# Reading a transposed activation tile from its SBUF copy instead of from PSUM, in an 8-core attention and FFN kernel

## The reference

```python
xn = _layernorm(x, axis=-1)                  # x: (2, 8192, 1024) f32
latent = xn @ Wc_down                        # 1024 -> 512
q  = latent @ Wq_up                          # 16 heads of 64
kv = latent @ Wkv_up                         # one shared k and v head of 64
att = softmax(causal(q k^T / 8))
s = (att v) @ Wc_proj
h = silu(xn @ wg^T) * (xn @ wu^T)            # weights int32, times 1/127; hidden 3072
g = _silu(h @ wd^T)
out = x + s * g
```

## Time and profile before

| | us |
|---|---|
| time before, median of 2 runs | 3452.53 (3451.27 to 3453.78) |
| the profiled execution's own time | 3440.83 |
| its span, slowest core (core 5) | 3439.2 |
| spans of the 8 cores | 3406.5 to 3439.2 |
| mean granted TensorE clock of the cores | 0.790 to 0.808 |

### The profile page before, as it was taken

How to read it: one execution, slowest core, us unless ns; L and a number is a source line. 1 busy time by engine, 2 the same in 40 slices (tenths; PEclk the granted TensorE clock), 3 DMA queues, 4 the chain that set the end, 5 groups by cost and what they waited for, 6 DMA issues and landing times.

```text
span 3439.2 us, 33260 instructions; the slowest of 8 cores (3406.5 to 3439.2 us)
## 1 busy us (share of the span) xinstructions
PE 2153.8 (63%) x10464; PEld 1011.4 (29%) x10464; DVE 1186.9 (35%) x1978; ACT 1307.1 (38%) x1457; POOL 414.6 (12%) x329
## 2 busy tenths in 40 slices
PE   1334645466565574775748747587575787577876
PEld 1112323222231341442225222252221442223521
DVE  3635443342433435324243242432322322421221
ACT  0111222212331332433534436444455336366455
POOL 0111212222233001000000000000000001000000
PEclk9556767776887797997879978799787799689998
DMA  5032254839576143351015300153001251011510
GB/s 89 27 54 49 37 88 60 128 71 148 60 86 113 43 119 112 69 133 42 28 39 123 100 14 26 37 130 94 13 17 42 46 148 38 14 33 33 140 44 13
DMA packets 547288, 232.14 MB, mean 67 GB/s; under 512 B 476464, under 2 KB 532784, under 8 KB 547120
## 3 DMA queue, kind: packets, MB, share of 16 engines
q1 hardware_dynamic: 429792, 186.88, 21.0%
q0 software_dynamic: 117328, 43.14, 11.8%
HBM read 241.62 MB, written 27.26 MB: 78 GB/s over the span
## 4 chain that ended last, share of the span: by engine, by line
PE 39%; DVE 20%; DMA 15%; issue 11%; ACT 10%; POOL 4%; DVEq 1%; SPq 0%; ACTq 0%; POOLq 0%
PE ps_y L553 9%; PE ps_sc L566 9%; ACT p_sb L577 8%; PE ps_u L724 5%; PE ps_u L731 4%; POOL p_sb L585 4%; PE ps_u L795 3%; DMA wu_t<-wu 3%; DMA wd_t<-wdbf 3%; DVE recbf L605 3%; DMA xt<-xb 3%; DMA wd_t<-wd 2%; PE ps_u L643 2%; DVE xnT_own L390 2%; DVE stat L302 2%
## 5 line engine op out<-in xcount | busy, mean ns | idle before, releaser
L577 ACT ACTIVATE p_sb<-ps_sc 128x1024 bf16<-128x1024 f32 x1088 | 1088.9, 1022 | 1556.4 <-PE ps_sc L566 1549.8
L553 PE MATMUL ps_y<-p_sb,vaug_sb 128*65 128x512 bf16 x2176 | 758.5, 434 | 244.7 <-POOL p_sb L585 143.4
L566 PE MATMUL ps_sc<-qs,kT_sb 65*128 65x512 bf16 x2176 | 755.3, 433 | 26.9 <-DVE qs L534 26.9
L585 POOL TENSOR_TENSOR p_sb<-p_sb,masks_sb 128x1024 bf16<-128x1024 bf16 x128 | 275.0, 2158 | 2440.0 <-ACT p_sb L577 2439.8
L553 PEld LDWEIGHTS ps_y<-p_sb,vaug_sb 128*65 128x65 bf16 x2176 | 220.1, 122 | 684.0 <-issue 611.2
L369 PE MATMUL ps_u<-ident_sb,xn_t 128*128 128x128 bf16 x512 | 67.5, 278 | 454.9 <-DVE xn_t L332 238.9
L795 PE MATMUL ps_u<-wd_t,h_sb 128*128 128x512 bf16 x768 | 219.9, 419 | 153.5 <-DMA wd_t<-wdbf 61.3
L566 PEld LDWEIGHTS ps_sc<-qs,kT_sb 65*128 65x128 bf16 x2176 | 223.8, 108 | 241.1 <-issue 99.4
L724 PE MATMUL ps_u<-xnT_own,wg_t 128*128 128x256 bf16 x1536 | 226.9, 297 | 81.9 <-DVE h_sb L742 59.7
L595 DVE CAST yf<-ps_y 64x1024 bf16<-64x1024 f32 x32 | 38.8, 1214 | 590.3 <-PE ps_y L553 590.3
L731 PE MATMUL ps_u<-xnT_own,wu_t 128*128 128x256 bf16 x1536 | 216.6, 288 | 14.7 <-DMA wu_t<-wu 14.4
(11 more groups left out here) (85 smaller groups left out, 1270.5 us busy)
## 6 DMA issues: line engine op xcount, KB each, us to landing
wg_t<-wgbf SPq DMA_DIRECT2D x144, 256.0 KB, 3.5
wu_t<-wubf SPq DMA_DIRECT2D x144, 256.0 KB, 4.0
wd_t<-wdbf SPq DMA_DIRECT2D x288, 128.0 KB, 2.2
xt<-xb SPq DMA_DIRECT2D x64, 512.0 KB, 4.6
wg_t<-wg POOLq DMA_DIRECT2D x48, 256.0 KB, 7.5
wu_t<-wu POOLq DMA_DIRECT2D x48, 256.0 KB, 8.5
wd_t<-wd POOLq DMA_DIRECT2D x96, 128.0 KB, 3.9
xo_t<-xo SPq DMA_DIRECT2D x16, 512.0 KB, 4.2
```

What stands on the lines that cost most here:

```text
L553: last = O("tensor", lambda e_, t=t, nh=nh, par=par: e_.matmul(ps_y[0:65, nh * 512:(nh + 1) * 512], vaug_sb[:, t, :], p_sb[:, par, nh * 51 ...
L566: sct = O("tensor", lambda e_, t=t, nh=nh, sb2=sb2: e_.matmul(ps_sc[:, sb2 * 1024 + nh * 512:sb2 * 1024 + (nh + 1) * 512], kT_sb[0:65, t * ...
L577: ex = O("scalar", lambda e_, sb2=sb2: e_.activation(p_sb[:, sb2, :], ps_sc[:, sb2 * 1024:(sb2 + 1) * 1024], AF.Exp), [sct, st["p_war"][sb ...
L585: mtoks[t] = O("gpsimd", lambda e_, pview=pview, mj=mj: e_.tensor_tensor(pview, pview, masks_sb[:, mj, :].unsqueeze(1).broadcast_to([128, ...
```

## The change

The accumulate takes its input from `xnT`, the bf16 copy that the cast has just written in SBUF, and no longer from `ps_u`, f32 in PSUM. It therefore waits for the cast (`ev`) in place of the last transpose matmul. `st["util"]` stays the cast's token. Since the accumulate now reads `xnT`, the layernorm of a later tile with the same half of `xnT` also carries the token of that accumulate (`xnacc`) among its waits. The values differ in one thing: the factor is applied to a value already rounded to bf16; with factors 1 and 0 the result is the same.

```diff
+            "xnacc": [None, None],
...
             if acc is not None:
                 q, g = acc
                 dstv = xnT_own[:, :, g * 128:(g + 1) * 128]
-                srcv = ps_u[:, :].rearrange("p (k n) -> p k n", k=DK)
                 if q == 0:
-                    a2 = O("vector", lambda e, dstv=dstv, srcv=srcv, q=q:
+                    a2 = O("vector", lambda e, dstv=dstv, srcv=dst_ap, q=q:
                            e.tensor_scalar_mul(dstv, srcv, sel_sb[:, q:q + 1]),
-                           [mts[-1], st["xnown_war"], t_misc], out="v")
+                           [ev, st["xnown_war"], t_misc], out="v")
                 else:
-                    a2 = O("vector", lambda e, dstv=dstv, srcv=srcv, q=q:
+                    a2 = O("vector", lambda e, dstv=dstv, srcv=dst_ap, q=q:
                            e.scalar_tensor_tensor(dstv, srcv, sel_sb[:, q:q + 1],
                                                   dstv, ALU.mult, ALU.add),
-                           [mts[-1], st["xnown_war"], t_misc], out="v")
+                           [ev, st["xnown_war"], t_misc], out="v")
                 st["xnown_war"] = a2
-                st["util"] = a2
+                st["xnacc"][q % 2] = a2
                 if q == 3:
                     xown_done[g] = a2
...
             submit_ln(xt[:, par, :], xn_t[:, xpar, :],
                       xnT[:, 0, :, (j % 2) * 128:(j % 2) * 128 + 128],
-                      [dma, st["xn_war"][xpar], st["xnT_war"]], done_aff, done_tp,
-                      flush=flush, acc=(j % 4, j // 4))
+                      [dma, st["xn_war"][xpar], st["xnT_war"], st["xnacc"][j % 2]],
+                      done_aff, done_tp, flush=flush, acc=(j % 4, j // 4))
```

## The result

| | before | changed |
|---|---|---|
| median of the executions, us | 3449.5 (10 runs) | 3351.1 (11 runs) |
| ratio, compared executions | | 0.9698 (95% interval 0.9669 to 0.9728) |
| the same on two more chips | | 0.976 (0.972 to 0.980), 0.9715 (0.9693 to 0.9736) |
| profiled execution, us | 3440.8 | 3356.1 |
| spans of the 8 cores, us | 3406.5 to 3439.2 | 3318.9 to 3354.3 |

The kernel is 3.0% faster in the first comparison: 0.9698 x 3449.5 = 3345 us, a gain of 104 us. (The ratio leaves out executions in which one die ran at a lower granted clock; the medians in the first row take them in.) The forecast was 3378 us with a range down to 3348. The interval of the ratio is 3335 to 3356 us, so the low end of the range lies inside the measurement's own uncertainty.

A forecast was written before the change was run, and what follows sets the result against it. No single engine bounds the kernel; it is a string of handoffs in fixed order. Terms: 72.9 - 0.5 - 4 - 2 + 8 = 74.4 us off the median 3452.5 gives 3378 us, range 3348 to 3405.

The forecast's parts named there:

- The handoffs: At TensorE's waits for the accumulate: release by the cast takes some 1.17 to 1.2 us off each, 72.9 us.
- What it adds: On VectorE: the accumulate starts 0.24 us later and still takes 1.27 us, nearly all hidden; 0.5 us charged.
- the size of the cover: Slot 14, accumulate's start to next cast: 3.07 us left after the change, against 1.51 us needed.
- The shortfall of 0.16 us at the start: At the kernel's start, without attention between: cover of 1.35 us is 0.16 short, three places, 0.5 us in all.
- Both engines at SBUF: Slots 1 to 4, accumulate meeting GpSimd mask product: up to 1.9 us on VectorE, 0.6 on GpSimd; 4 us charged.
- Handed on: In slots reading int32 weights: TensorE, now ahead, meets a load on its way in places; 2 us charged.
- The clock: Closed gaps bring the higher clock level a little sooner: 8 us gained, bounds -20 to +20 us.
- the clock's larger gift: Rival: two more 3 us at the higher level in each of 15 slots, 45 us more, 3341 us; chance 0.18.
- 2% slower: Rival: accumulates meet mask products at nearly all 48, 3480 us; over 2% needs twice the price per meeting, chance 0.01.
- The signs: Expected in the trace: accumulate waits gone, second-tile waits 1.2 us shorter, block at 0.85 us, accumulate out of the chain.
- VectorE's idle before the next cast: Sign on VectorE: this idle would become some 1.4 us shorter than before.
- The clock moves by over 0.02: Sign against the forecast: it would be wrong if the granted clock moved by more than 0.02.

The follow-up runs named there:

- the run that puts it back: Changed kernel with ps_u again free only when the accumulate has ended, the accumulate still reading SBUF; ratio to the kernel before 1.0028.
- the run without it: Changed kernel without the 48 accumulates L390, each group's first tile copied as it is; ratio to the kernel before 0.9733.
- the doubled accumulate: Changed kernel with a second, equal operation behind each of the 48 L390, writing to a scratch tile; ratio to the kernel before 0.9825.
- the fill: Kernel before with two extra 512-column matmuls in front of each key/value block and each group's fourth tile, nothing released earlier; ratio 0.9929.
- the order of two layernorms: Changed kernel with, from slot 2 on, the second pair's layernorm written behind the first pair's key/value block and transposes some steps later; ratio to the kernel before 0.9343.

## Where the prediction was right, and which step failed

**The handoffs.** Right, in place and in size. Slot 0's own group, four handoffs and no attention between, went from 23.19 to 18.45 us: 4.74 us, 1.185 for each, where the sum had 1.17 and 1.18. The release is the whole of it, as the run that puts it back shows.

**What it adds.** Right where it mattered. L390's price is 1.285 us (taken 1.27); L386's is 0.486, near the lower bound, and the changed kernel gains nothing by it. The accumulate lies under cover: the run without it gains 5 us. But the size of the cover was read at the low clock, and the doubled accumulate cost 24 to 29 us for the 5 to 20 that I gave it. The shortfall of 0.16 us at the start didn't appear.

**Both engines at SBUF.** Right and small. The longest L390 takes 1.742 us, so a meeting cost VectorE 0.5 us at most and not 1.9. Two of the meetings on the timeline:

```profile
127.26 2.11 POOL L585 TENSOR_TENSOR p_sb<-p_sb,masks_sb 128x1024 bf16<-128x1024 bf16 x1 [7.25 <-ACT p_sb L577]
128.71 1.74 DVE L390 SCALAR_TENSOR_TENSOR xnT_own<-xnT,sel_sb,xnT_own 128x1024 bf16<-128x1024 bf16 x1
...
274.03 1.28 DVE L390 SCALAR_TENSOR_TENSOR xnT_own<-xnT,sel_sb,xnT_own 128x1024 bf16<-128x1024 bf16 x1 [0.46 <-DVE xnT L377]
274.37 5.00 POOL L585 TENSOR_TENSOR p_sb<-p_sb,masks_sb 128x1024 bf16<-128x1024 bf16 x2 [39.73 <-ACT p_sb L577]
```

The mask products of the changed kernel, by the page's groups (line, shapes, count, busy us, mean ns, idle before),

```profile
L585 POOL TENSOR_TENSOR p_sb<-p_sb,masks_sb 128x1024 bf16<-128x1024 bf16 x128 | 277.6, 2179 | 2366.8 <-ACT p_sb L577 2366.7
```

sum to 277.6 us, for 275.0 in the kernel before. I charged 4 us, it was about 3 on GpSimd. There are five meetings on each core. In one the accumulate comes second and takes 1.74 us for 1.285; in four the mask product comes second and takes 2.57 to 3.00 us for 2.115 (the 5.00 us above are one of 2.92 us and one of the usual length, which meets nothing). The one that comes second is held each time, for the rest of the first less 0.1 to 0.2 us. So the trace agrees with the page of the Trainium skill that the prediction had put beside it (SBUF — State Buffer, "Who interferes with whom"), by which the two exclude each other. The 1.9 us had been read where VectorE arrives at the start of a mask product; here it came second once, with 0.66 us of the product left.

**Handed on.** Groups 1 to 3 saved 9.3 us in place of 14, and from the stretches' 90.4 us to the mean span's 84.4 (3420.9 to 3336.5) another 6 are lost between the stretches: about 11 us, charged at 2 + 4.

**The clock: the step that failed.** The prediction put +8 us for the clock, and for the bounds one 3 us stretch more or less at the high level in each of 15 slots. In groups 4 to 15 a stretch became 30.3 - 24.0 = 6.4 us shorter, of which four handoffs are 4.7. The other 1.6 us, 12 x 1.6 = 20 us, came at a share of 0.928 for 0.830. That is a remainder; that it is the clock's is borne out by the fill, 1.34 us a stretch at 0.898 with no handoff moved, and by the release put back, some 0.6 us a stretch lost at 0.785 beyond its waits. So the term was 20 us and not 8: as large as its upper bound. It was priced as a share of one more 3 us at the high level, from one place in slot 14, where the high level was rare (6.8 of 28 us). Behind the second cast the change closed three gaps of 1.2 us: idle time of TensorE in gaps over 0.5 us fell from 5.5 to some 2 us a stretch. It shortened the wait of 10 us before the second tile by as much. With that the time at the low level fell from 8.8 to 3.0 us.

With 72.9 + 20 - 11 the sum is 82 us, for 84 in the traces' mean span; taken from 3452.5 that is 3370 us, inside the range. So of the 30 us by which the forecast fell short the clock explains 12, less some 4 that the losses were charged too low. What put the measured time outside the range is the other 20 or so, and their cause stays open. Part of it is the draw: the profiled execution before was 6 to 9 us under its kernel's median and the one after 5 over it, so that pair shows 85 us on the slowest core where the timed executions show 82 to 104.

**The range.** Its low end, 3348, is a gain of 104 us from 3452.5: 67 us and 38 of the 45 that the clock's larger gift was priced at. It left nothing for the slowest core or for the uncertainty of a comparison, some 10 us either way in the first. Two workings in the prediction don't come out: half of the larger gift is 67 + 22.5 = 89.5 us, 3363 and not 3355; and for 2% slower a meeting would have to cost (69 + 72.9) / 48 = 3.0 us, 1.4 times the 2.1 and not twice. Neither moves the forecast.

**The signs.** TensorE's waits, the 1.37 us, the 0.85 us to the block and the chain came as told. VectorE's idle before the next cast did not: 2.38 us for 2.97, so 0.6 less and not 1.4, since L386 is 0.79 us shorter. No accumulate came near 3 us. "The clock moves by over 0.02" was too coarse a sign: its mean over the whole span and all cores moved from 0.801 to 0.809, while in the stretches it moved by a tenth.

## What to carry to other kernels

In an order fixed by hand a shared PSUM tile should be released by the first operation that has copied it, and every other reader should read the copy; what it is worth is the number of waits that end on the late reader times the start-to-start time that goes, and idle times before a matmul group understate it. When a change closes short gaps in a stretch where TensorE is otherwise busy, read the granted clock there in every slot and not in one, let the sum reach to what it gives if the high level is held nearly throughout, and read every cover at that level too. Then look at what the long waits end on: here the order of two layernorms was worth more than the release.

## What the runs showed of the hardware

Two added matmuls in a gap of 1.2 us made a kernel 0.7% faster (0.9929), by way of the granted clock (0.830 to 0.898 in the stretches). A fill of 28 matmuls in a wait of 10 us gave nothing, neither where it left 3.8 us of idle behind it nor where it ran 2.0 us past the wait (0.9723, against 0.9715 and 0.976 without it). A product with a factor and a bf16 result took 0.486 us for 128x1024 from bf16 in SBUF, for 1.275 from f32 in PSUM; with an added second stream, 1.285 us from SBUF and 1.275 from PSUM: for that operation the source made no difference. Where such an operation with two streams from SBUF and a GpSimd product of the same size met, the one that came second was held, five times of five (1.74 us for 1.285; 2.57 to 3.00 for 2.115).
